# A fused two-layer attention and expert kernel: the routing before the first experts and the opening steps of the second attention are put in another order

## The reference

```python
x = x + tanh(g_xattn[0]) * L0_xattn(layernorm(x), ctx, ctx)        # softmax over the query axis
x = x + tanh(g_ffn[0])   * L0_ffn(layernorm(x))                    # 8 experts, hidden 1024, top 2
x = x + tanh(g_xattn[1]) * L1_xattn(layernorm(x), ctx)             # self and context attention, gated
x = x + tanh(g_ffn[1])   * L1_ffn(layernorm(x))                    # 15 experts, hidden 512, top 3, one shared
```

## Time and profile before

| | us |
|---|---|
| median of 3 runs | 1229.87 (1229.16 to 1230.22) |
| the profiled execution, its own time | 1233.03 |
| its span in the profile | 1231.3 |
| PE busy in it | 1169.8 (95%) |
| DVE, ACT, POOL busy | 595.4, 479.4, 391.7 |

### The profile page before, as it was taken

The page is one execution under the profiler, slowest core; times in us unless marked ns, Lnnn a source line. Parts: engine busy times, 40 slices in busy tenths (PEclk is TensorE's granted clock), DMA queues, the critical chain, the costliest instruction groups (busy, mean ns, idle before and its releaser), DMA issues. The chain is left out here.

```text
span 1231.3 us, 29193 instructions
## 1 busy us (share of the span) xinstructions
PE 1169.8 (95%) x11425; PEld 901.6 (73%) x11425; DVE 595.4 (48%) x1437; ACT 479.4 (39%) x1130; POOL 391.7 (32%) x411
## 2 busy tenths in 40 slices
PE   6999999977999999998799999999998999999998
PEld 4767777756999999974466666666665579999975
DVE  5777777774210001057566666567656612111226
ACT  3545555523323332324445444444454232233221
POOL 3666666632223222131101011010011245555420
PEclk9999999977999999999899999999999999999999
DMA  6011111305999998640021000000000459999965
GB/s 182 24 28 36 28 37 44 122 15 190 383 325 337 316 341 315 250 135 19 2 87 30 16 21 21 26 9 9 2 9 14 165 196 349 350 360 353 341 224 168
DMA packets 64392, 180.93 MB, mean 147 GB/s; under 512 B 10176, under 2 KB 36608, under 8 KB 55808
## 3 DMA queue, kind: packets, MB, share of 16 engines
q1 hardware_dynamic: 55088, 156.40, 36.9%
q0 software_dynamic: 8064, 22.03, 5.0%
q10 hardware_dynamic: 1104, 0.64, 0.2%
HBM read 163.11 MB, written 15.93 MB: 145 GB/s over the span
## 5 line engine op out<-in xcount | busy, mean ns | idle before, releaser
L2301 ACT ACTIVATE ex_hT<-kept_psum,ex_w 128x128 f32<-128x128 f32 x464 | 132.9, 369 | 294.8 <-PE kept_psum L2356 157.4
L2356 PE MATMUL kept_psum<-ex_xT,ex_w 128*128 128x128 f32 x1856 | 222.5, 276 | 0.0
L2356 PEld LDWEIGHTS kept_psum<-ex_xT,ex_w 128*128 128x128 f32 x1856 | 215.7, 193 | 0.1
L2367 PE MATMUL kept_psum<-ex_w,ex_hT 128*128 128x256 f32 x928 | 214.0, 379 | 0.0
L2263 DVE TENSOR_TENSOR ex_yt<-kept_psum,ex_b 128x256 f32<-128x256 f32 x84 | 35.7, 425 | 353.6 <-PE kept_psum L2367 353.6
L2367 PEld LDWEIGHTS kept_psum<-ex_w,ex_hT 128*128 128x128 f32 x928 | 170.1, 190 | 19.8
L2229 POOL DMA_INDIRECT ex_results<-ex_yt,ex_to_row x84 | 83.0, 988 | 254.9 <-DVE ex_yt L2263 254.9
L1249 ACT ACTIVATE at_probs<-kept_psum 120x800 f32<-120x800 f32 (+2 forms) x128 | 101.3, 842 | 85.5 <-PE kept_psum L1418 85.5
L1088 DVE TENSOR_REDUCE at_negmax<-kept_psum 100x2 f32<-100x722 f32 x128 | 115.5, 902 | 0.0
L568 ACT ACTIVATE at_probs<-kept_psum 120x800 f32<-120x800 f32 (+1 forms) x96 | 80.1, 837 | 73.7 <-PE kept_psum L691 73.6
L410 DVE TENSOR_REDUCE at_negmax<-kept_psum 120x8 bf16<-120x800 f32 (+1 forms) x96 | 90.6, 985 | 23.4 <-PE kept_psum L682 23.0
(11 more groups left out here) (252 smaller groups left out, 1691.1 us busy)
## 6 DMA issues: line engine op xcount, KB each, us to landing
ex_w<-in_pack_in SPq DMA_DIRECT2D x32, 1028.0 KB
ex_w<-in_pack_out SPq DMA_DIRECT2D x32, 1024.0 KB
ex_w<-in_pack_in SPq DMA_DIRECT2D x52, 514.0 KB
ex_w<-in_pack_out SPq DMA_DIRECT2D x52, 512.0 KB
at_ctx<-in_ctxT SPq DMA_DIRECT2D x31, 361.0 KB, 3.6
ex_normed<-ex_xhat SPq DMA_DIRECT2D x16, 200.0 KB
ex_w<-ex_results SPq DMA_DIRECT2D x6, 400.0 KB
ex_sw<-in_L_ffn_sW SPq DMA_DIRECT2D x2, 1024.0 KB
```

The costliest lines, as they stand in the source:

```text
L2301: last = act.activation(hT[t % N][:, c, :], ps_h[:, (t * U + u) % N, i * P:(i + 1) * P], ACT.Gelu, bias=w1[t % N][:, B1 + c:B1 + c + 1])
L2356: last = pe.matmul(ps_h[:, (t * U + u) % N, i * P:(i + 1) * P], w1[t % N][:, c * ff + f:c * ff + f + P], xT[t % N][:, c, :], start=(c == 0 ...
L2367: last = pe.matmul(ps_y[:, t % N, 0:D], hT[t % N][:, c, :], w2[t % N][:, c * D:(c + 1) * D], start=(c == 0), stop=(c == FC - 1))
```

## The change

1. *End of `attend0`.* The residual of batch 14 comes before `select`; `select` for the first 12 batches is cut in two, choice 0 at step 16 and choice 1 with the mask at step 17; `lanes` moves to step 18. The 24 `in_lanes` instructions of these batches go: DVE makes plain one-hots for choice 0 in one instruction of 12x128 elements (`hot_lanes`), and for choice 1 the same later, in the experts' program; POOL multiplies each by the token number, 1536 elements in one instruction (`number_lanes`). PE runs `late_tensor` before `rank_up` at step 17. Two times four idle products are added at the last step.
2. *Start of the first experts.* `expert_of` is computed after `in_lanes` and not in `starts`. PE issues 15 idle products after `tabulate`.
3. *Opening of `attend1`.* The own projection of batch 0 is written in two banks, the half that the first two score units need first, and ACT takes it in halves with a semaphore of its own; that of batch 1 moves behind the first score unit. `moments(1)` and the four `fed.vector` calls move later (group 1 to step 0, group 2 to step 1, group 3 to step 2). Step 1 gets an order of its own like that of the light steps (own projection behind the third key unit, own values before the fourth). The handover inside the attention moves from step 2 to step 3. Idle products are shifted and some added.
4. *Memory.* The two `probs` tiles swap places; `w1` of the second experts is allocated earlier.

```diff
         for t in range(B + 4):
             if t == B:
                 prep.normed(dve, PAIRED - 2)
-                prep.route.select(dve, 0)
             if on(t - 2):
                 residual(t - 2)
+            if t == B:
+                prep.route.select(dve, 0, range(1))
...
             if t == B + 1:
+                prep.route.select(dve, 0, range(1, 2))
+            if t == B + 2:
                 prep.route.lanes(dve, 0)
-            if t == B + 2:
-                prep.route.in_lanes(dve, 0)
+                prep.route.hot_lanes(dve, 0, 0)
...
+            if t == LAST:
+                keep_warm(into("sum", LAST - 1), 4)
...
+            if t > B:
+                late_tensor(pe, prep, psum, t)
             if t == B + 1:
                 prep.route.rank_up(pe, 0)
-            if t > B:
-                late_tensor(pe, prep, psum, t)
...
+        def hot_lanes(dve, i, k):
+            b0, b1 = SPLIT[i]
+            dve.tensor_tensor(in_lane[:, k * B + b0:k * B + b1, :], minus_lanes[0:T, :].unsqueeze(1).to_broadcast([T, b1 - b0, P]),
+                              lane_of[:, k, b0:b1].unsqueeze(2).to_broadcast([T, b1 - b0, P]), ALU.is_equal).then_inc(hot_ready, 1)
+
+        def number_lanes(pool, i, k):
+            b0, b1 = SPLIT[i]
+            pool.wait_ge(hot_ready, k + 1)
+            columns = in_lane[:, k * B + b0:k * B + b1, :]
+            pool.tensor_tensor(columns, columns, tok[:, b0:b1].unsqueeze(2).to_broadcast([T, b1 - b0, P]), ALU.mult).then_inc(lanes_ready[i], 1)
+
+        def experts_of(dve):
+            last = E - 1
+            then(dve.tensor_tensor(passed[:, :, 0:last], cols[0:1, 0:TILES].unsqueeze(2).to_broadcast([1, TILES, last]),
+                                   end[0:1, 0:last].unsqueeze(1).to_broadcast([1, TILES, last]), ALU.is_ge))
+            then(dve.tensor_reduce(expert_f[:, :], passed[:, :, 0:last], AX, ALU.add))
+            dve.tensor_scalar(expert_of[:, 0:NT], expert_f[:, :], float(last), None, ALU.min).then_inc(expert_ready, 1)
...
+            if not shared:
+                for k in range(top):
+                    route.number_lanes(pool, 0, k)
...
                 route.spread(dve)
+                route.hot_lanes(dve, 0, 1)
             route.starts(dve)
             route.lanes(dve, last)
             route.in_tiles(dve)
             route.in_lanes(dve, last)
+            if not shared:
+                route.experts_of(dve)
...
             if early is not None:
                 early.tensor_done(pe)
+                for _ in range(15):
+                    pe.matmul(ps_t[:, 1, 0:P], ident[:, :], early.wa[:, 0, 0:P], start=True, stop=True)
```

The opening of the second attention:

```diff
+    NO_VALUES_ORDER = (("max", 0), ("key0", 4), ("key1", 4)) + LIGHT_ORDER[3:]
+    LIGHT, NO_VALUES = range(B - NK + 1, B - 1), range(1, 2)
...
-        moments(1)
-        fed.vector(dve, 1)
         for t in STEPS:
-            if t == 3:
+            if t == 4:
                 second.enter(dve)
...
             if t == 0:
+                moments(1)
+            if t == 1:
+                fed.vector(dve, 2)
+            if t == 2:
+                fed.vector(dve, 3)
+                fed.finished(dve)
+            if on(t + 1):
+                maxima(t + 1, 1)
+            if t == 0:
                 newton(1)
                 normed(2)
-            if on(t + 1):
-                maxima(t + 1, 1)
...
             if t == 0:
-                fed.vector(dve, 2)
+                fed.vector(dve, 1)
...
+        def take_first_own():
+            act.wait_ge(masks_set, 4)
+            for i, name in enumerate(("own", "own_more")):
+                act.wait_ge(ready[name], 1)
+                bank = ring_bank(name, 0)
+                act.activation(kT[0][:, i, 0:T], bank[:, (KC + i) * T:(KC + i + 1) * T], ACT.Identity, bias=bqk[:, KC + i:KC + i + 1])
+                for a in range(2):
+                    last = act.activation(qz[0][:, i, a, :], bank[:, i * T:(i + 1) * T], ACT.Identity, bias=bqm[:, i, a:a + 1],
+                                          scale=own[:, a:a + 1]).then_inc(first_own_taken, 1)
...
-        project_own(0)
-        project_own(1)
-        keep_warm(psum[:, 2, :], 2)
+        project_first_own()
...
             if on(t + 1):
                 by_query(t + 1, 0)
+            if t == -1:
+                project_own(1)
             if t == 0:
                 turn_max(t)
+                keep_warm(into("xT", 2), 5)
...
-            if x_batch(t) is not None and t not in LIGHT:
+            if x_batch(t) is not None and not spread_out(t):
                 project_own(x_batch(t))
             if on(t):
                 by_key(t, 2)
-            if x_batch(t) is not None and t in LIGHT:
+            if x_batch(t) is not None and spread_out(t):
                 project_own(x_batch(t))
...
-            if t in LIGHT:
+            if spread_out(t):
                 values_own(t)
```

More of the change, by code:

```diff
@@ L624, in into, with keep_warm @@
             return ring_bank(name, b)
+        def keep_warm(bank, n):
+            for _ in range(n):
+                pe.matmul(bank[:, 0:P], ident[:, :], wk[:, 0, 0:P], start=True, stop=True)
         def transposes(b):
@@ L1023, in gpsimd @@
         root(0)
-        fed.gpsimd(pool, 0)
+        for g in range(NG):
+            fed.gpsimd(pool, g)
         root(1)
-        for g in range(1, NG):
-            fed.gpsimd(pool, g)
         for b in range(B + 4):
-            if b == 2:
+            if b == 3:
                 second.clear(pool)
@@ L1210, in vector @@
                 residual(t - 2)
-            if on(t) and t not in LIGHT:
+            if on(t) and not spread_out(t):
                 take_value_own(t)
-            if t == 1:
-                fed.vector(dve, 3)
-                fed.finished(dve)
+            if t == 2:
                 second.leave(dve)
@@ L1375, in project_own, with project_first_own @@
             last.then_inc(ready["own"], 1)
+        def project_first_own():
+            pe.wait_ge(taken["xT"], 1)
+            for i, name in enumerate(("own", "own_more")):
+                bank = into(name, 0)
+                for part in (i, KC + i):
+                    for c in range(KC):
+                        last = pe.matmul(bank[:, part * T:(part + 1) * T], w[:, c, part * P:(part + 1) * P], xT[0][:, c, :],
+                                         start=(c == 0), stop=(c == KC - 1))
+                last.then_inc(ready[name], 1)
         def by_query(b, u):
             scores_free("q", b, u)
+            if b == 0:
+                pe.wait_ge(first_own_taken, u + 1)
             if u == 0:
-                pe.wait_ge(taken["own"], b + 1)
+                if b > 0:
+                    pe.wait_ge(taken["own"], b + 1)
                 if b < KEYED:
@@ L1619 @@
     in_lanes: Callable
+    hot_lanes: Callable
+    number_lanes: Callable
+    experts_of: Callable
     starts: Callable
@@ L1847, in routing, with select @@
         table = psum[:, 3, 0:top * TILES]
-        def select(dve, i):
+        def select(dve, i, ks=range(top)):
             b0, b1 = SPLIT[i]
@@ L1985, in raise_up @@
                 act.activation(sel[:, :, :], key[:, :, :], ACT.Exp).then_inc(exp_out, 1)
-        return Routing(select, rank_up, lanes, in_lanes, starts, in_tiles, tabulate, rows, weigh, spread, raise_up,
+        return Routing(select, rank_up, lanes, in_lanes, hot_lanes, number_lanes, experts_of, starts, in_tiles, tabulate, rows, weigh, spread, raise_up,
                        lane_at, expert_of, expert_ready, from_ready, rows_ready)
```

66 lines of the change are left out of this document (39 added, 27 removed).

## The result

The changed kernel takes 1234.55 us (median of 22 runs, 1230.61 to 1239.67) against 1231.38 before (22 runs): ratio 1.003, 95% interval 1.0019 to 1.004. It is 2.3 to 4.9 us slower, where 1220.3 and a gain of 10 us were forecast. The profiled execution (1233.50 us, span 1231.8) lies 1 us under its median, and the one of before 1.7 above its own, so the two traces differ by only 0.5 us, and the runs by 3.2. What follows reads places inside the traces, and leaves sums to the runs.

The account below looks back on a forecast made before the run. PE, busy 95% of the span, was taken as the bound. Routing's 0.8 loss and the opening's 10.5 gain took the profiled 1233.03 to 1223.3, or 1220.3 us as median, range 1214.5 to 1225.5.

Parts of the forecast that it names:

- Opening: Start of the second attention: reordered steps win 10.5 us, bounds 8 to 11.5, with first maxima turned 1.5 earlier.
- Step 1: Second attention: new order removes PE waits and low clock, 23.80 us becomes 18.9, a gain of 4.9.
- Step 2: Second attention: `fed.vector(3)` moves between maxima units, 27.20 us becomes 23.0, a gain of 4.2.
- (e) The handover goes to step 3 ... hidden: Second attention: the handover's memsets and second experts' loads, needed over 200 us later, cost nothing in step 3.
- The last logits ... 3.1 earlier: End of the first attention: last logits taken at about 274.9, from the residual's new place (2.3) and better clock (1.5).
- The hold: First experts' `starts`: POOL's multiplications, 3.3 us each, hold DVE's two-input L1924 until 286.4 instead of 284.63.
- w1 later ... cost nothing, covered by the gather: First experts: later `expert_of` delays w1's load, asked for at 291 to 292, there at 297; uncovered, up to 1.5 us.
- first `hidden`: First experts: low clock after PE's pause makes it take 5.28 us, not 3.74, ending at 303.8: 0.8 later.
- `from_row` 1.4 to 1.7 later: First experts' routing: the row that issues the gather is written at 292.7 to 293.0, because POOL holds DVE.
- the four: Rivals: DVE not held, 1214.9 (0.15); POOL slower, middle 1225 (0.10); opening given back, 1226.5 (0.10); other side (0.05).
- The opening's gain is given back: Second attention: DVE late at maxima, new PE waits of 2 to 3 us, steps win only about 3; 1226.5, chance 0.10.
- The one on the other side: Routing: POOL's `number_lanes`, two in series, so slow that the opening's 10.5 is lost; 10 us each gives 1233; chance 0.05.

Follow-up runs that it names:

- routing_only: Only the edits outside `attend1`, earlier `w1` among them, second attention as before, against the kernel before: 1236.94 us, ratio 1.0045.
- experiment 5, loads_later: Changed kernel with the second experts' five loads a step later and ACT's bias scaling two steps later: 1236.32 us, ratio to before 1.004.
- experiment 6, no_idle: Changed kernel without the 23 idle products of the last step and the first experts' start: 1230.55 us, ratio to before 0.9995.
- experiment 7, opening_pad: Kernel before with the opening and memory changes, plus 23 idle products where PE awaits the first gathered rows: 1227.65 us, ratio to before 0.9968.
- experiment 9, loads_later5: Changed kernel with the second experts' loads in step 4 and ACT's bias scaling in step 5: 1229.87 us, ratio to before 0.9977.
- Experiment 3, early_experts: Changed kernel with the three `expert_of` instructions back inside `starts`: 1231.44 us, ratio to before 0.9994.
- mends 3 and 4: Changed kernel with `expert_of` back inside `starts` (1231.44 us), and, separately, with the multiplication by token numbers on ACT instead of POOL (1230.50 us).
- act_numbers: Changed kernel with the multiplication by token numbers on ACT in place of POOL: 1230.50 us, ratio to before 0.9994.
- opening_only: Only the `attend1` edits, the swapped `probs` tiles and the earlier `w1`, against the kernel before: 1223.56 us, ratio 0.9935.
- pad_later5: Kernel before with opening and memory changes, 23 idle products at the first gather, second experts' loads in step 4, scaling in step 5: 1223.28 us, ratio 0.9933.
- act_early_later, experiment 8: Changed kernel with numbers on ACT, `expert_of` inside `starts`, second experts' loads a step later, scaling two later: 1230.13 us, ratio to before 0.9994.
- act_early_later5: Changed kernel with numbers on ACT, `expert_of` inside `starts`, second experts' loads in step 4, scaling in step 5: 1223.89 us, ratio to before 0.9941.
- act_spread: Changed kernel with numbers on ACT, second dozen split around the fourth key, `expert_of` in `starts`, loads in step 4, scaling in step 5: 1221.76 us, ratio 0.9928.

## Why the prediction was wrong

The forecast for the profiled execution was 1223.3, and 1233.50 was measured, 10.2 more. Three places hold nearly all of it: the start of the second attention came 5.9 us later and not 0.8 (5.1), step 3 lost 4.2 where nothing was put down, and the opening won 10.1 and not 10.5 (0.4). In the medians the miss is 14.3: the forecast took before for 1229.87, a median of 3 runs (22 runs give 1231.38), and took the changed kernel's profile to lie 3.2 above its median, as that of before did, when it lies 1 under it.

By its own steps:

- **Opening, right.** First maxima turned 1.5 earlier: measured 1.6 (565.07 - 551.74 = 13.33 against 14.95 before). Step 0 nothing: 0.3 won. Step 1 18.9: 19.0. Step 2 23.0: 23.8. Sum 10.5: 10.1. Part of the agreement in step 1 is luck. In `routing_only` the old step 1 ran at full clock and took 21.3, not 23.8, while its step 0 took 21.2, not 20.4; so 1.6 of the 10.1 us hang on where the clock was low in the one trace of before. In the runs the opening alone wins 7.8 (6.4 to 9.6), less than 10.5.
- **"(e) The handover goes to step 3 ... hidden", wrong, 4.2 us.** The working asked who needs the loads, and found nobody for 200 us. It did not ask what else uses the transfer engines: the blocks of instructions. The stall of 1.56 us cost more than its length: 2.6 with the unit it cuts, and 1.6 by the clock that fell behind it. Experiments 5, 6, 7 and 9 show the two conditions: the place in PE's list, and the loads running then. That PE's next block of instructions is what came late is the explanation that fits both; it is not seen directly. The stall is also why the halves (-2.2 in sum) do not add up to +3.2: of the difference of 5.4, 4.2 is the stall's, and 1.2 is less than the scatter of three medians.
- **"The last logits ... 3.1 earlier", wrong by 3.8 us.** They came 0.7 later. I had put 1.5 on the clock of the last step and 2.3 on the residual's place. The residual of batch 15 starts at 270.25, as before (270.31), and half of `select` now stands behind it. Over all profiled executions here that moment scatters, from 266.95 to 273.54 in the eight with edit 1 whole (mean 269.7) and from 268.51 to 273.14 in the four with the old code (mean 270.3): 3.8 was to be won and 0.6 is seen, inside the scatter. The clock is the reason that the trace gives. The residual's place did what it should: PE's wait before the last output projection fell from 2.73 to 0.55. But in the changed kernel 64 records of the last values (L724) took 2.90 us at the low level, against 1.59 before. The dip had lain at 250 to 260 us, and had only moved to 261 to 267.
- **The hold, right in kind, undersized.** The forecast had one hold of 1.8 us, on L1924, and the first multiplication past before DVE had anything with two inputs to do. But that one met `select`, and the second L1995: 2.4 + 2.6 = 5.0 us, though POOL took 2.75 for each and not 3.3. The Trainium skill's rule ("SBUF — State Buffer", Who interferes with whom) holds in both rows.
- **"w1 later ... cost nothing, covered by the gather", wrong, about 2 us.** By the working's own sum `expert_of` is written just ahead of `from_row`, at about 292.6, and in the trace of before SP issues the load 1.0 behind it (285.88 to 286.86): the load would have been asked for at about 293.6, together with the gather, and not at 291 to 292. And it was priced as something the gather hides. The two share the transfer engines, and the gather is what PE waits for: 5.85 us for 3.7. Experiment 3: 3.1 us. The slow first `hidden` was forecast (5.28, measured 5.36).
- **`from_row` 1.4 to 1.7 later: 3.8; first `hidden` 0.8 later: 6.3.** The routing alone costs 5.6 us in the runs. The mends 3 and 4 give 3.1 and 4.1 by themselves and 6.0 together (1229.87 - 1223.89). The chain without the scatter ahead of it, from the start of the last residual to `from_row`, in each profiled execution (that of `act_numbers` aside):

| | us |
|---|---|
| old routing: before, `opening_only`, `opening_pad`, `pad_later5` | 20.9, 20.9, 20.3, 20.2 |
| changed routing: changed kernel, `routing_only`, `loads_later`, `loads_later5`, `no_idle` | 24.8, 24.8, 24.8, 24.8, 24.8 |
| `early_experts` | 25.4 |
| numbers on ACT: `act_early_later`, `act_early_later5`, `act_spread` | 22.4, 22.3, 21.4 |

So the changed routing is 4 us longer than the old one in this chain alone, and still 0.5 to 1.2 longer with every mend.
- **Rivals.** None of the four named what happened. "The opening's gain is given back" comes nearest, but not through DVE's waits. The one on the other side was built on a slow POOL, and POOL was faster than forecast. Three mechanisms of 3 to 5 us each made the sum turn: the hold, the collision of load and gather, and the stall, which needs both halves of the change.

What stays open: whether PE's stall is a late block of instructions, as argued; whether the new order of `select` and the residual and the eight idle products of the last step win anything; 0.6 us inside a scatter of 6 does not tell, and no experiment undid them alone. Nor was it tried where the limit of the late block lies, in instructions or in bytes of loads.

## What to carry to other kernels

- Price a moved transfer by what shares the transfer engines at its new time, a gather that an engine waits for and the engines' own instructions included, and not only by who needs its data. A wait of "issue" in the middle of one line of matmuls, while a large load runs, is a reason to suspect a late block of instructions. Move the load, or shift PE's list by some instructions, and see whether the wait goes; here both removed it.
- Elementwise work that is moved to POOL can hold DVE (here 2.57 and 2.80 us for 0.2): count every DVE instruction with two SBUF inputs that can start while POOL runs, for the earliest and the latest time it may start. ACT did the same work in 3.6 us a dozen without holding DVE, but PE then waited 2.03 us for a key behind it.
- When halves that were measured alone do not add up to the whole, look for the place that has changed in the whole only.

## What the runs showed that was not expected

- 23 small matmuls, some 340 us upstream, decided whether PE stood still for 1.56 us (and lost 4.2) in a stage that they do not touch: `opening_only` 22.9 us in step 3, `opening_pad` 27.1.
- A gather of 128 rows took 3.7 us with the first weights on their way for 5.5 us, 3.0 us with them 6.4 us ahead (experiment 8, from 291.92 to 294.92), and 5.85 us when both were issued within 0.03 us of each other. All traces fall the same way: 3.0 to 3.7 us in the five with the loads 5.5 to 6.4 us ahead and PE waiting for the gather, 5.3 to 5.85 in the five with both issued together.
